# Message passes of a four-layer GNN: matrix building before the segment sums in PE's turn

## The chip, the cores and the metric

The kernel runs on one core of one Trainium2 chip. The metric is the time of one execution on the device, in microseconds (us). Lower is better. A core has five engines that work side by side and are ordered only by semaphores: TensorE (PE; the profile lists its weight loads apart, as PEld), VectorE (DVE), ScalarE (ACT), GpSimd (POOL) and SyncE (SP). Each runs its own instructions strictly in the order in which the kernel wrote them.

## The reference

A graph with 6250 nodes of 64 features and 206250 edges, sorted by destination, goes through four layers. Each normalizes the rows, applies relu, and adds the layer's result to x.

```python
h = relu(layernorm(x))
# L0: agg[dst] += h[src] @ W_msg + b_msg ; out = l2norm(agg + h @ W_self + b_self)
# L1: out[dst] += h[src] @ weight[edge_type]            (16 relations)
# L2: three hops: emb' [dst] += edge_weight * emb[src]  ; out = mean of the four emb
# L3: e = mlp(h_src, h_dst, edge_attr) ; out[dst] += e * (h @ W_src)[src] ; out += h @ W_tgt
```

So L0 and L1 each need one message pass: fetch a row of a table for every edge, and add the rows of the edges of one destination (a segment sum). L2 needs the same sparse matrix three times. The kernel therefore builds it once as dense chunks in DRAM (`B_d`) and multiplies by it.

## The kernel before

Edges lie in steps of 128 edges of one destination block. Eight steps (G = 8) are a group. A pass over all edges is 208 groups, 52 iterations of R = 4 turns, one group a turn. There are two message passes (0 for L0, 1 for L1), and in their turns the chunks of the L2 matrix are built as well. A chunk has 16 parts. Pass 0 builds 39 chunks with 3 parts in each of its 208 turns. Pass 1 builds the other 23 chunks with 2 parts in each of its first 184 turns. Its last 24 turns build nothing.

What one turn of group g consists of, engine by engine, each in this order in its own queue:

- POOL (`rows_of_group`, L497): waits for the group's indices (`idx_ok`), then issues eight indirect DMAs that gather 128 rows each into slot r of four in `gat`. After one turn in sixteen parts it also fetches a record for the matrix (`matrix_rows`, L506).
- PE (`segment.groups`, L884): waits for the group's gathers, for its one-hot matrix S (`S_ok`), and for the sum bank to be free (`acc_ok`), makes eight matmuls S x rows into bank 6 or 7 (16 instructions in the profile), and signals `mm_ok`. Then come the turn's matrix parts (`matrix_part`, L871): eight matmuls each (again 16 instructions), which wait for `lhs_ok` from DVE and, for the bank, for `bev` from ACT. Once a chunk, three transposes follow (`record_columns`, L862).
- DVE: the one-hot matrix of group g+1 (`one_hot`, L1190, which waits until segment sum g-1 is done), then for each part three instructions (`matrix_part`, L1228, L1229, L1231, the last one signals `lhs_ok`; the first waits until the matmuls of the part before last are done), once a chunk `record_weights` (L1209 to L1214), then `accumulate` (L1204): a wait for `mm_ok` of group g and eight additions of the sum bank into the accumulators.
- ACT: waits for `mm_ok` of group g and copies the indices of group g+4 for POOL (L683), then empties the banks of the turn's parts into `stg` (`matrix_part`, L671), once a chunk `columns_of` (L662).
- SP writes `stg` to `B_d` in quarters of a chunk (`matrix_out`, L420).

The order in each queue is written out by hand. `message_turns` runs all engines through the same turns: eight iterations (pass 0) or four (pass 1) are written out as one loop body. Between the passes `project` (L842) makes the second table.

Of the kernel before, what the change touches and what calls it, by code (L numbers as in the profile page):

```python
# [21 lines left out]
def gnn_kernel(nc, x, src, dst, edge_attr, etype, eweight, msg_wt, msg_b, self_wt, self_b, lin, rel_w,  # L22
# [51 lines left out]
    with ExitStack() as ctx:  # L74
# [207 lines left out]
        def wait(eng, semaphore, value):  # L282

            if not isinstance(value, int) or value > 0:
                eng.wait_ge(semaphore, value)
# [8 lines left out]
        def message_turns(n, eng, body):  # L294

            size, turn = BODY[n], PER_TURN[n]
            per_body = size * R * turn // SUBS

            def parts(b, k):
                at = [[(k * R + r) * turn + t for t in range(turn)] for r in range(R)]  # L300
                return [[(b * per_body + (FIRST[n] + o // SUBS), o % SUBS, (FIRST[n] + o // SUBS) % 2) for o in row] for row in at]

            def whole(b, count):
                for k in range(count):
                    body(b * size + k, parts(b, k))

            whole(0, size)
            with eng.Fori(1, BUILD_ITERS[n] // size) as b:
                whole(b, size)
            whole(BUILD_ITERS[n] // size, BUILD_ITERS[n] % size)  # L310
            if BUILD_ITERS[n] < ITER:
                none = [[] for r in range(R)]
                with eng.Fori(BUILD_ITERS[n], ITER - 1) as i:
                    body(i, none)
                body(ITER - 1, none)

        def next_chunk(row, pos):

            for c, at, h in row:
                if at == pos and not (isinstance(c, int) and c == NCH - 1):  # L320
                    return c + 1, 1 - h
            return None
# [221 lines left out]
        def _(act):  # L544
            parts = [0]
# [112 lines left out]
            def columns_of(c, h):  # L658

                act.wait_ge(s_["recT"], c + 1)  # L660
                wait(act, s_["lhs_ok"], (c - 1) * SUBS)
                act.copy(cols[:, h, :], ps[1][:, 0:3 * P]).then_inc(s_["cols_ok"], 1)  # L662

            def matrix_part(c, pos):

                act.wait_ge(s_["bmm"], c * SUBS + (pos + 1))
                r, j = pos // QS, pos % QS
                if j == 0:
                    wait(act, b_out[r % 2], c * 32 + r // 2 * 16)
                w = G // 2 * KC  # L670
                act.copy(stg[:, r % 2, j * w:(j + 1) * w], ps[3 + j % 2][:, 0:w]).then_inc(s_["bev"], 1)  # L671

            def message_pass(n, table):

                for r in range(R):
                    act.wait_ge(s_["mm_ok"], n * NG + r + 1)
                    act.copy(idx[:, r, :], table[:, r * G:(r + 1) * G]).then_inc(s_["idx_ok"], 1)

                def groups(i, parts):
                    for r in range(R):  # L680
                        if not (isinstance(i, int) and i == ITER - 1):
                            act.wait_ge(s_["mm_ok"], i * R + (n * NG + R + r + 1))
                            act.copy(idx[:, r, :], table[:, bass.ds((i * R + (R + r)) * G, G)]).then_inc(s_["idx_ok"], 1)  # L683
                        for c, pos, h in parts[r]:
                            matrix_part(c, pos)
                        ahead = next_chunk(parts[r], 9)
                        if ahead:
                            columns_of(*ahead)

                message_turns(n, act, groups)  # L690
# [95 lines left out]
        def _(pe):  # L786
# [69 lines left out]
            def record_columns(c, h):  # L856

                pe.wait_ge(s_["wm_ok"], c + 1)
                wait(pe, s_["cols_ok"], c)
                for f in range(3):  # L860
                    g0 = (0, 1, 3)[f] * P
                    ins = pe.transpose(ps[1][:, f * P:(f + 1) * P], recb[:, h, g0:g0 + P], ident[:])  # L862
                ins.then_inc(s_["recT"], 1)

            def matrix_part(c, j):

                pe.wait_ge(s_["lhs_ok"], c * SUBS + (j + 1))
                wait(pe, s_["bev"], c * SUBS + (j - 1))
                for t in range(G):
                    a, i2 = t % 2, t // 2  # L870
                    ins = pe.matmul(ps[3 + j % 2][a * KP:(a + 1) * KP, i2 * KC:(i2 + 1) * KC], Lw[:, j % 2, t, :], Rc[:, j % 2, t, :],  # L871
                                    start=True, stop=True)
                ins.then_inc(s_["bmm"], 1)

            def segment(n):

                def groups(i, parts):
                    for r in range(R):
                        pe.wait_ge(gather_ok[r], i * (16 * G) + (n * (NG // R) + 1) * 16 * G)
                        pe.wait_ge(s_["S_ok"], i * R + n * NG + r + 1)  # L880

                        wait(pe, s_["acc_ok"], (i * R + n * NG + r - 1) * G)
                        for k in range(G):
                            ins = pe.matmul(ps[6 + r % 2][:, k * D:(k + 1) * D], S[:, r % 2, k, :], gat[:, r, k * D:(k + 1) * D],  # L884
                                            start=True, stop=True)
                        ins.then_inc(s_["mm_ok"], 1)
                        for c, pos, h in parts[r]:
                            matrix_part(c, pos)
                        ahead = next_chunk(parts[r], 9)
                        if ahead:  # L890
                            record_columns(*ahead)

                message_turns(n, pe, groups)
# [518 lines left out]
```

## Time and profile before

| | |
|---|---|
| median of 3 runs | 8440.53 us (8440.46 to 8444.3) |
| profiled execution | 8453.61 us, span 8451.6 us, mean granted clock 0.665 |
| PE busy | 5784.8 us, 68% of the span |
| DVE busy | 4682.9 us, 55% |
| POOL busy | 4978.6 us, 59% |
| ACT busy | 1528.8 us, 18% |

The profile describes one execution. Busy times are sums over the span, so an engine that is the limit of one stage may look idle in the mean. The two message passes take slices 2 to 12 and 13 to 23 of the profile's 40 slices of 211 us each. A granted clock of 0.5 is TensorE's level of 1.2 GHz, 1.0 is 2.4 GHz, and values between are mixtures over the stretch.

### The profile page before, as it was taken

What the parts mean: (1) busy time and instruction counts of PE and PEld (TensorE: products, weight loads), DVE (VectorE), ACT (ScalarE), POOL (GpSimd) and SP (SyncE); (2) the same over time, 40 slices, a digit from 0 to 9 for tenths busy, and PEclk for the clock granted to TensorE, in tenths of its full rate; (3) what the DMA queues carried; (4) which work ended last, traced back from release to release, by engine and by line L of the source; (5) the groups of instructions that cost most, each with busy time, mean ns of one, the idle gap of its engine ahead of it and who ended that gap; (6) DMA issues with size and microseconds to landing.
All of it is one profiled execution on the core that took longest, in us unless ns stands there. A gap on an engine that the chain in (4) does not pass through costs nothing.

```text
span 8451.6 us, 133532 instructions
## 1 busy us (share of the span) xinstructions
PE 5784.8 (68%) x42197; PEld 4230.0 (50%) x42197; DVE 4682.9 (55%) x10280; ACT 1528.8 (18%) x4330; POOL 4978.6 (59%) x5265
## 2 busy tenths in 40 slices
PE   2476777777776555556554477777767788778877
PEld 2466666666644555555554222222235555555555
DVE  3688898998863667667664200000025555555555
ACT  1111111111122111111110000000013333333333
POOL 0577777777733777777777411111117777777776
PEclk6566556555555666666665699999976656665666
DMA  5655555555543444444442599999953333333332
GB/s 135 97 92 89 89 93 91 92 93 89 90 101 106 71 68 71 68 69 69 68 71 42 201 426 401 423 426 397 426 217 87 82 82 82 81 82 82 82 81 69
DMA packets 794607, 1178.96 MB, mean 139 GB/s; under 512 B 619664, under 2 KB 647729, under 8 KB 766544
## 3 DMA queue, kind: packets, MB, share of 16 engines
q1 hardware_dynamic: 616460, 919.49, 35.5%
q0 software_dynamic: 172528, 250.20, 16.2%
q8 instruction: 215, 3.52, 0.2%
q10 hardware_dynamic: 5204, 4.11, 0.2%
q14 instruction: 200, 1.64, 0.1%
HBM read 921.76 MB, written 258.23 MB: 140 GB/s over the span
## 4 chain that ended last, share of the span: by engine, by line
POOL 45%; issue 20%; DMA 16%; PE 12%; DVE 5%; ACTq 1%; DVEq 1%; POOLq 0%; ACT 0%; SPq 0%
POOL arena L497 44%; DMA arena<-B_d 12%; PE ps L931 5%; DMA arena<-tab,idx 2%; PE ps L842 2%; PE ps L884 2%; DVE ps L1228 1%; ACTq L279 1%; DMA arena<-rec_d,tcol 1%; DVE arena L1231 1%; DVE pair L1204 1%; PE ps L871 1%; PE ps L835 1%; DVE arena L1229 1%; POOL recb L506 1%
## 5 line engine op out<-in xcount | busy, mean ns | idle before, releaser
L497 POOL DMA_INDIRECT arena<-tab,idx x4992 | 4730.9, 948 | 1907.9 <-issue 1644.1
L884 PE MATMUL ps<-arena 128*128 128x64 f32 x6656 | 1351.6, 388 | 1088.0 <-DMA arena<-tab,idx 1010.2
L884 PEld LDWEIGHTS ps<-arena 128*128 128x128 f32 x6656 | 1288.0, 297 | 1172.0 <-issue 921.0
L871 PE MATMUL ps<-arena 128*64 128x98 f32 x15872 | 1368.0, 349 | 447.0 <-DVE arena L1231 440.3
L871 PEld LDWEIGHTS ps<-arena 128*64 128x64 f32 x15872 | 1152.4, 206 | 610.8 <-DVE arena L1231 548.0
L931 PE MATMUL ps<-arena,ev 128*64 128x512 f32 (+1 forms) x4836 | 1106.7, 603 | 370.8 <-DMA arena<-B_d 294.9
L1229 DVE TENSOR_TENSOR arena<-arena,ps 128x784 f32<-128x784 f32 x992 | 957.1, 965 | 0.0
L931 PEld LDWEIGHTS ps<-arena,ev 128*64 128x64 f32 x4836 | 383.9, 143 | 1093.3 <-issue 742.4
L534 POOL DMA_INDIRECT ev<-emb_d,dvI x186 | 175.1, 941 | 1259.5 <-PE ps L931 1041.4
L1190 DVE TENSOR_TENSOR arena<-relT,ps 128x1024 f32<-128x1024 f32 x624 | 759.3, 1217 | 201.7 <-issue 198.8
L1296 DVE COPY pair<-ps 128x512 f32<-128x512 f32 x9 | 5.7, 684 | 1437.4 <-PE ps L931 1437.4
L1228 DVE TENSOR_TENSOR ps<-arena,ps 128x512 f32<-128x512 f32 x992 | 682.7, 688 | 157.6 <-PE ps L871 155.9
L671 ACT COPY stg<-ps 128x392 f32<-128x392 f32 x992 | 481.3, 485 | 1426.7 <-PE ps L871 1411.7
L958 PE MATMUL ps<-ident,arena 128*64 128x128 f32 x3328 | 384.9, 406 | 446.7 <-DMA arena<-tab,idx 446.7
L1231 DVE TENSOR_TENSOR arena<-ps,arena 128x512 f32<-128x512 f32 x992 | 679.2, 685 | 5.3 <-issue 5.3
L958 PEld LDWEIGHTS ps<-ident,arena 128*64 128x64 f32 x3328 | 303.1, 209 | 708.1 <-DMA arena<-tab,idx 705.9
L1359 DVE TENSOR_TENSOR pair<-pair,ps 64x128 f32 x1664 | 475.2, 286 | 212.3 <-PE ps L993 121.2
L1204 DVE TENSOR_TENSOR X<-X,ps 128x64 f32 x832 | 183.8, 221 | 723.3 <-PE ps L884 698.0
L1204 DVE TENSOR_TENSOR pair<-pair,ps 128x64 f32 x2496 | 515.6, 220 | 69.7 <-issue 51.1
L1331 DVE TENSOR_TENSOR arena<-ps,stg 128x512 f32<-128x512 f32 x208 | 143.9, 692 | 660.7 <-ACT stg L759 657.0
L752 ACT COPY arena<-arena 128x192 bf16 x1664 | 440.4, 347 | 126.4 <-issue 126.4
L954 PE MATMUL ps<-stg,Web 17*128 17x512 f32 x416 | 350.1, 933 | 29.1 <-DMA stg<-attr_s 29.1
(213 smaller groups left out, 3889.2 us busy)
## 6 DMA issues: line engine op xcount, KB each, us to landing
arena<-B_d SPq DMA_DIRECT2D x186, 3136.0 KB, 17.2
B_d<-stg SPq DMA_DIRECT2D x248, 784.0 KB
arena<-tab,idx POOLq DMA_INDIRECT x4992
arena<-rel_d SPq DMA_DIRECT2D x208, 256.0 KB
tab<-arena SPq DMA_DIRECT2D x26, 1024.0 KB, 3.8
attr_s<-arena SPq DMA_DIRECT2D x13, 512.0 KB, 14.6
stg<-attr_s SPq DMA_DIRECT2D x208, 32.0 KB
emb_d<-pair SPq DMA_DIRECT2D x3, 1664.0 KB, 16.3
```

What stands on the lines that cost most here:

```text
L497: pool.indirect_dma_start(gat[:, r, k * width:(k + 1) * width], None, table, bass.IndirectOffsetOnAxis(ap=idx[:, r, k:k + 1], axis=0)).the ...
L671: act.copy(stg[:, r % 2, j * w:(j + 1) * w], ps[3 + j % 2][:, 0:w]).then_inc(s_["bev"], 1)
L871: ins = pe.matmul(ps[3 + j % 2][a * KP:(a + 1) * KP, i2 * KC:(i2 + 1) * KC], Lw[:, j % 2, t, :], Rc[:, j % 2, t, :], start=True, stop=True)
L884: ins = pe.matmul(ps[6 + r % 2][:, k * D:(k + 1) * D], S[:, r % 2, k, :], gat[:, r, k * D:(k + 1) * D], start=True, stop=True)
L931: ins = pe.matmul(ps[k][h * D:(h + 1) * D, 0:n], ev[:, u % EVS, :], Bb[:, u % BUFS, c0:c0 + n], start=c == 0, stop=c == NCH - 1)
L958: pe.matmul(ps[h][t * D:(t + 1) * D, q * P:(q + 1) * P], gv[:, r, k, D:2 * D], ident[:], start=False, stop=True, skip_group_check=True)
L1190: dve.tensor_tensor(S[:, h, :, :], steps_of(relT, g), iota_view(n, P), ALU.is_equal).then_inc(s_["S_ok"], 1)
L1204: dve.tensor_tensor(a, a, ps[6 + r % 2][:, k * D:(k + 1) * D], ALU.add).then_inc(s_["acc_ok"], 1)
L1228: dve.tensor_tensor(ohp, column(0, KP), iota_view(0, KP), ALU.is_equal).then_inc(s_["ohp_ok"], 1)
L1229: dve.tensor_tensor(Rc[:, j % 2, :, :], column(1, KC), iota_view(0, KC), ALU.is_equal)
L1231: dve.tensor_tensor(Lw[:, j % 2, :, :], ohp, column(2, KP), ALU.mult).then_inc(s_["lhs_ok"], 1)
L1359: dve.tensor_tensor(a, a, part, ALU.add).then_inc(s_["acc_ok"], 1)
```

## The change

In each turn of both message passes PE now makes the turn's matrix parts first and the group's segment sum after them. ACT empties the banks of these parts first, and waits for the segment sum and copies the indices after that. The orders of DVE, POOL and SP stay. No instruction is added or removed.

```diff
@@ ScalarE, groups(i, parts) @@
                     for r in range(R):
+                        for c, pos, h in parts[r]:
+                            matrix_part(c, pos)
                         if not (isinstance(i, int) and i == ITER - 1):
                             act.wait_ge(s_["mm_ok"], i * R + (n * NG + R + r + 1))
                             act.copy(idx[:, r, :], table[:, bass.ds((i * R + (R + r)) * G, G)]).then_inc(s_["idx_ok"], 1)
-                        for c, pos, h in parts[r]:
-                            matrix_part(c, pos)
                         ahead = next_chunk(parts[r], 9)
@@ TensorE, groups(i, parts) @@
                     for r in range(R):
+                        for c, pos, h in parts[r]:
+                            matrix_part(c, pos)
                         pe.wait_ge(gather_ok[r], i * (16 * G) + (n * (NG // R) + 1) * 16 * G)
                         pe.wait_ge(s_["S_ok"], i * R + n * NG + r + 1)
...
                         ins.then_inc(s_["mm_ok"], 1)
-                        for c, pos, h in parts[r]:
-                            matrix_part(c, pos)
                         ahead = next_chunk(parts[r], 9)
```

## Rows read from the trace of the kernel before

**Rows 1.** The page, busy tenths and granted clock in 40 slices.

```profile
DVE  3688898998863667667664200000025555555555
POOL 0577777777733777777777411111117777777776
PEclk6566556555555666666665699999976656665666
```

**Rows 2.** Source view of the gathers, pass 0: count, ns min/median/max, first and last start.

```profile
L497 POOL DMA_INDIRECT arena<-tab,idx x1664: 940/944/1058, 287.4 to 2412.3; - x185
```

**Rows 3.** The same for pass 1.

```profile
L497 POOL DMA_INDIRECT arena<-tab,idx x1664: 940/944/1062, 2635.4 to 4738.7; - x185
```

**Rows 4.** Timeline of pass 0 (start, us, engine, line; idle before).

```profile
2001.08 1.65 DVE L1204 TENSOR_TENSOR pair<-pair,ps 128x64 f32 x8
2002.72 3.68 PE L884 MATMUL ps<-arena 128*128 128x64 f32 x16
...
2009.44 0.69 DVE L1231 TENSOR_TENSOR arena<-ps,arena 128x512 f32<-128x512 f32 x1
...
2010.18 0.89 PE L871 MATMUL ps<-arena 128*64 128x98 f32 x16 [0.50 <-DVE arena L1231]
2010.25 1.66 DVE L1204 TENSOR_TENSOR pair<-pair,ps 128x64 f32 x8
...
2011.00 2.00 PE L884 MATMUL ps<-arena 128*128 128x64 f32 x16
...
2020.82 1.65 DVE L1204 TENSOR_TENSOR pair<-pair,ps 128x64 f32 x8 [0.95 <-issue]
```

**Rows 5.** Timeline of pass 1, two turns.

```profile
3402.77 3.67 PE L884 MATMUL ps<-arena 128*128 128x64 f32 x16 [8.99 <-DMA arena<-tab,idx]
...
3406.66 0.22 DVE L1204 TENSOR_TENSOR X<-X,ps 128x64 f32 x1 [7.00 <-PE ps L884]
...
3415.56 0.22 DVE L1204 TENSOR_TENSOR X<-X,ps 128x64 f32 x1 [0.96 <-issue]
...
3421.96 0.69 DVE L1231 TENSOR_TENSOR arena<-ps,arena 128x512 f32<-128x512 f32 x1
```

**Rows 6.** Timeline of pass 0, parts spaced by DVE.

```profile
1926.78 1.57 PE L871 MATMUL ps<-arena 128*64 128x98 f32 x16 [0.96 <-DVE arena L1231]
...
1928.28 3.68 PE L884 MATMUL ps<-arena 128*128 128x64 f32 x16
...
1933.99 1.57 PE L871 MATMUL ps<-arena 128*64 128x98 f32 x16 [0.50 <-DVE arena L1231]
...
1936.07 1.28 PEld L871 LDWEIGHTS ps<-arena 128*64 128x64 f32 x16 [0.80 <-DVE arena L1231]
```

**Rows 7.** Windows: us, then busy of PE, PEld, DVE, ACT, POOL, granted clock.

```profile
1930.00:1940.00 10.00, 6.64 (x58) 5.59 (x57) 7.56 (x17) 1.65 (x4) 7.56 (x9) 0.50 0.58 97
2010.00:2020.00 10.00, 5.95 (x72) 5.20 (x74) 9.70 (x23) 1.86 (x5) 7.54 (x8) 0.83 0.70 108
4600.00:4700.00 100.00, 36.71 (x160) 34.88 (x160) 28.44 (x90) 1.97 (x10) 75.48 (x81) 0.50 0.15 26
```

**Rows 8.** Groups by line, pass 0 (299 to 2428 us).

```profile
L871 PE MATMUL ps<-arena 128*64 128x98 f32 x9984 | 891.3, 355 | 374.9 <-DVE arena L1231 368.8 <-ACT stg L671 4.1 <-issue 0.7
L884 PE MATMUL ps<-arena 128*128 128x64 f32 x3328 | 667.8, 384 | 199.6 <-DMA arena<-tab,idx 137.9 <-issue 36.6 <-DVE arena L1190 16.1
...
L1228 DVE TENSOR_TENSOR ps<-arena,ps 128x512 f32<-128x512 f32 x624 | 429.8, 689 | 157.6 <-PE ps L871 155.9
L1204 DVE TENSOR_TENSOR pair<-pair,ps 128x64 f32 x1663 | 331.9, 220 | 61.9 <-issue 51.1 <-DVE pair L1204 7.8
```

**Rows 9.** Groups by line, pass 1 while it builds (2647 to 4500 us).

```profile
L884 PE MATMUL ps<-arena 128*128 128x64 f32 x2928 | 592.1, 386 | 735.5 <-DMA arena<-tab,idx 720.3 <-DVE arena L1190 6.9 <-DVE pair L1204 6.1
L871 PE MATMUL ps<-arena 128*64 128x98 f32 x5854 | 473.6, 340 | 72.1 <-DVE arena L1231 71.5
...
L1190 DVE TENSOR_TENSOR arena<-relT,ps 128x1024 f32<-128x1024 f32 x183 | 223.3, 1220 | 33.4 <-issue 31.9
```

## The prediction

> **What bounds the kernel now.** I read the 40 slices first, then the gathers, then two turns of the timeline, then the groups of each pass.
>
> In the slices of pass 0 (2 to 12) POOL stands at 7 while DVE stands at 8 or 9; in pass 1 (13 to 23) POOL again at 7, DVE at 6 or 7, with a granted clock of 0.6 in both [rows 1]. POOL's 7 is a full engine: the reader is to see that gathers run without a hole. In pass 0 1664 gathers start between 287.4 and 2412.3 us, together with 39 record gathers on the same engine: 2124.9 / 1702 = 1.248 us from start to start, of which 0.94 is busy and the rest is issue [rows 2]. Pass 1: 2103.3 / (1663 + 23) = 1.247 us [rows 3]. So POOL paces both passes, with 8 x 1.248 = 9.98 us for a group.
>
> DVE is close behind in pass 0. From one run of additions (L1204) to the next it takes 2010.25 - 2001.08 = 9.17 us, and a turn with a record has 1.4 more (10.57) [rows 4]. What matters is how it gets there: its additions need the segment sum of the same turn, and PE had made that sum (2.00 to 3.68 us) while DVE was building the turn's parts. DVE never waits for L884 in pass 0: its L1204 shows 61.9 us of idle time, none of it put down to PE [rows 8].
>
> **The change part by part.** *PE's order.* Segment sum g now stands behind the parts of turn g, the last of which waits for DVE's last L1231 of the turn. DVE's next instruction after that L1231 is the additions of g, which wait for segment sum g. Behind these additions in DVE's queue stand the one-hot matrix and all parts of the next turn, so nothing else can fill the wait; PE in turn then waits for the first of those parts. The two engines that overlapped now take turns. A turn is then a loop of five terms:
>
> 1. DVE, from its first addition to the end of the last L1231. Pass 0: 2009.44 + 0.69 - 2001.08 = 9.05 us [rows 4]. Pass 1, with two parts: 3421.96 + 0.69 - 3415.56 = 7.09 us [rows 5].
> 2. From there to PE's start: 2010.18 - 2010.13 = 0.05 us [rows 4].
> 3. The last part, to the start of the sum: 1928.28 - 1926.78 = 1.50 us at 1.2 GHz [rows 6], 2011.00 - 2010.18 = 0.82 at 2.4 GHz [rows 4].
> 4. The sum: 3.68 us or 2.00 us [rows 4].
> 5. From its end to DVE's first addition: 3406.66 - 3402.77 - 3.67 = 0.22 us [rows 5].
>
> Terms 2 to 5 come to 5.45 us at the low level and 3.09 us at the high one. A turn is 14.50 or 12.14 us in pass 0, and 12.54 or 10.18 us in pass 1. All are above POOL's 9.98, so POOL leaves the path and waits for indices instead.
>
> *Which level.* In the stretch 1930 to 1940 the parts start 2.08 us apart (1933.99, 1936.07), PE is idle for 0.5 us before each, and the clock stays at 0.50 [rows 6, 7]. That is the pattern of every turn after the change, since DVE makes a part in 2.08 us and PE no longer has a sum to catch up behind. Ahead of the first part PE will now always be idle for about 0.22 + 1.71 + 1.13 + 2.08, some 5.1 us. The stretch 2010 to 2020, with 0.83, follows PE work without such holes: sum, part and part nearly back to back. Segment sums alone, 3.67 of every 10 us, stay at 0.50 [rows 7]. So I take nine turns in ten at the low level: 14.50 - 0.1 x 2.36 = 14.26 us in pass 0, 12.54 - 0.24 = 12.30 us in pass 1.
>
> The Trainium skill (TensorE: Matmul & The Clock Gate, the HAM clock gate) says that the throttled clock is the default and that sustained activity releases it. A turn's PE work will be some 9 us long with holes of only 0.5 us, so by that rule the sum at its end would run at 2.4 GHz. That is a result of its own, and it stands among the rivals; the row of 1930 to 1940 speaks against it.
>
> *Records.* In 39 turns of pass 0 and 22 of pass 1, `record_weights` and the wait behind it cost DVE 1.4 us today. Now they lie in DVE's wait of 3.1 to 5.5 us for PE: no cost. PE's transposes follow the sum and lie in its idle time. If PE were done earlier than that, they would cost 39 x 1.4 = 55 us; I count nothing.
>
> *Stalls that POOL's pace hid.* DVE has idle time that no semaphore ends: in pass 0 some 33 us beside the record turns, worked out as the 70 us on its rows of "issue" less 39 x 0.95; in pass 1 31 us, nearly all ahead of L1190 [rows 8, 9]. In a serial loop they count: +33 and +31. PE has 36.6 us of the kind ahead of L884 in pass 0 [rows 8]; they may count too or fall into its idle time. I count none and keep 37 us for the upper end.
>
> *What goes.* DVE's 155.9 us of waiting for the banks of parts (L1228 on L871), which come from PE standing at a late gather, and PE's 137.9 and 720.3 us of waiting for gathers [rows 8, 9], vanish. They bring nothing: POOL hid them, and what is late next is the DVE and PE loop.
>
> *ACT's order.* Indices for group g+4 still leave right after sum g, because ACT waits for `mm_ok` in either order and the parts' banks are by then empty but for the last, 0.5 us. POOL then needs 10 us plus landing, and the group is used more than three turns (over 37 us) later: hidden. It would cost only if the gathers needed more than that. The bounds are 0 and, if those 0.5 us fell on POOL's path in each of 408 turns, 200 us; they are hidden while a turn is longer than 9.98 us. Taken: 0.
>
> *Sum.* Pass 0: 208 x 14.26 + 33 = 2999 us against 2428 - 298 = 2130 before: +869. Pass 1: 184 x 12.30 + 31 = 2294 us for the turns that build. Of the last 24, four have their gathers ready and twenty are paced by POOL: 20 x 9.98 + 10 = 210. That is 2504 against 2103 before (2647 to 4750): +401. Everything else, the hops and the edge layer included, is untouched. In all +1270 on the profiled execution: 8453.6 + 1270 = 9724 us. The median of the runs is 13 us below the profiled time, so 9711; I say 9710 us.
>
> **The rivals.**
> *A, the clock as it is now.* If the clock keeps today's shares, the means of the groups hold: a sum takes 667.8 / 208 = 3.21 us and a part 1.43 in pass 0; 592.1 / 183 = 3.24 and 1.29 in pass 1 [rows 8, 9]. With 0.07 off the part as in term 3, turns are 9.05 + 0.05 + 1.36 + 3.21 + 0.22 = 13.89 and 11.82 us, the passes 2922 and 2416: +792 and +313, 9545 us. For it: one slice is much like another today. Against: today's high stretches need work that the new order spreads out.
> *B, every sum at 2.4 GHz.* 208 x 12.14 + 33 = 2558 and 184 x 10.18 + 31 + 210 = 2114: +428 and +11, 8880 us. For it: the long activity ahead of each sum. Against: the stretch at 0.50 that has just that spacing.
> *C, POOL still paces (not slower).* One mechanism: with parts first, a late gather no longer holds up the parts, DVE runs ahead of PE, and the four gather slots take up the rest, so that each turn stays at POOL's 9.98 us. The place is DVE's wait ahead of L1204. The price is the loop of five terms, and it decides from where that falls under 9.98 us. Then the time stays at 8440 us; the ends of the passes could bring some 10 us either way. For it: pass 1 at the high level is at 10.18, nearly there. Against: pass 0 is 2 us above at any level, and DVE's queue leaves nothing to run ahead with. For the whole kernel it needs terms 3 and 4 to vanish.
>
> **How the numbers follow.** Forecast 0.70 (9600 to 9840 us on its own: all turns at the low level with PE's stalls is 208 x 14.50 + 33 + 37 = 3086 and 184 x 12.54 + 31 + 210 = 2548, so +956 and +445, 9841). A 0.19, between 9450 and 9600. B 0.08, C 0.03. The range that leaves out about two in ten, from the low side of A to the all-low sum, is 9450 to 9840 us. Against C this makes slower 0.97, same 0.02, faster 0.01. (0.2%, 17 us, is about what a measurement of this kernel can tell from no change.)
>
> **What would show it.** Right: in pass 0, DVE's L1204 waits for PE's L884 in nearly all 208 turns, some 4 to 5.4 us each, near 1000 us in all; PE's L871 waits for DVE's L1231 with one gap of about 5 us and two of 0.5 us a turn; POOL's L497 shows 4 us of idle time a turn ended by ACT's index copy, and PE no longer waits for gathers; the clock in slices of pass 0 reads 5, not 6. The first L1204 of two turns stand about 14.3 us apart in pass 0 and 12.3 in pass 1, and the last 24 turns stay at 10.0. The hops and the edge layer keep their lengths. Wrong: if the passes are long but L1204 does not wait for L884, the loop is another; if PE waits for gathers while POOL waits for indices, the four slots are too few; if the clock reads 6 or more, A or B.

## The result and the profile after

The changed kernel takes 9659.63 us (median; 9657.76 to 9662.04) against 8440.78 us: the ratio is 1.1443, with a 95% interval of 1.1423 to 1.1463. The profiled execution has a span of 9660.2 us at a mean clock of 0.616. The forecast was 9710 us, in a range of 9450 to 9840.

First the 40 slices of the page; one slice is now 241.5 us.

```profile
DVE  3566666666666445555555552000001555555555
POOL 0555555555555056566655665111110677777776
PEclk6555555555555555555555555999998666666666
```

POOL has gone from 7 to 5 and 6 and DVE from 8 or 9 to 6 in pass 0 [rows 1]: no engine is full in the passes any more, which is how a chain that goes back and forth between engines looks. The slices of the hops (9) and of the edge layer (6) read as before.

The clock's digits say little: in pass 0 the kernel before already reads 5 in eight of its eleven slices, and 6 in three [rows 1]; the changed kernel reads 5 throughout both passes. The windows of both (third figure from the right, the kernel before first) show that the granted clock fell from 0.60 to 0.54 in pass 0. In the building turns of pass 1 it fell from 0.62 to 0.51.

```profile
300.00:2428.00 2128.00, 1567.19 (x13429) 1391.36 (x13428) 1886.36 (x3898) 361.25 (x867) 1597.61 (x1693) 0.60 0.56 90
```
```profile
300.00:3200.00 2900.00, 1633.68 (x13246) 1423.13 (x13247) 1872.88 (x3859) 357.91 (x858) 1590.26 (x1685) 0.54 0.32 66
```

The source view of DVE's additions gives the ends of both passes and what they waited for. The kernel before, pass 0, then pass 1 with its last turns (count; ns min/median/max; first and last start):

```profile
L1204 DVE TENSOR_TENSOR pair<-pair,ps x1663: 209/220/223, 307.0 to 2427.9; 128x64 f32 x185
```
```profile
L1204 DVE TENSOR_TENSOR X<-X,ps x832: 209/222/223, 2650.4 to 4749.2; 128x64 f32 x167
  PE ps L884: 698.0, 125
```

The changed kernel, pass 0 and pass 1:

```profile
L1204 DVE TENSOR_TENSOR pair<-pair,ps x1664: 214/221/223, 301.6 to 3223.7; 128x64 f32 x185
  PE ps L886: 1015.0, 208
...
L1204 DVE TENSOR_TENSOR X<-X,ps x832: 213/221/223, 3446.0 to 5960.1; 128x64 f32 x167
  PE ps L886: 1123.6, 208
```

Pass 0 grew from 2120.9 to 2922.1 us (+801.2) and pass 1 from 2098.8 to 2514.1 (+415.3). The start is 5.4 us earlier. That makes +1211 of the +1208.6 us between the spans; all else stayed within 3 us. DVE waits for the segment sum (L886, formerly L884) in all 208 turns of each pass. It never did so in pass 0 before [rows 8], and 125 times in all before.

Two turns of pass 0 after, a selection of rows from the timeline (start, us; idle time before, and what ended it):

```profile
1802.22 0.68 DVE L1231 TENSOR_TENSOR arena<-ps,arena 128x512 f32<-128x512 f32 x1
1802.95 1.57 PE L871 MATMUL ps<-arena 128*64 128x98 f32 x16 [0.50 <-DVE arena L1231]
1804.46 3.68 PE L886 MATMUL ps<-arena 128*128 128x64 f32 x16
1808.37 1.65 DVE L1204 TENSOR_TENSOR pair<-pair,ps 128x64 f32 x8 [5.47 <-PE ps L886]
...
1813.41 1.58 PE L871 MATMUL ps<-arena 128*64 128x98 f32 x16 [5.28 <-DVE arena L1231]
1815.48 1.57 PE L871 MATMUL ps<-arena 128*64 128x98 f32 x16 [0.50 <-DVE arena L1231]
1816.83 0.68 DVE L1231 TENSOR_TENSOR arena<-ps,arena 128x512 f32<-128x512 f32 x1
1817.56 1.56 PE L871 MATMUL ps<-arena 128*64 128x98 f32 x16 [0.50 <-DVE arena L1231]
1819.05 2.00 PE L886 MATMUL ps<-arena 128*128 128x64 f32 x16
1821.28 1.66 DVE L1204 TENSOR_TENSOR pair<-pair,ps 128x64 f32 x8 [2.93 <-PE ps L886]
```

Read it as one chain: DVE's last L1231 ends at 1802.90, PE's last part starts 0.05 us later, the sum behind it ends at 1808.14, DVE's additions start at 1808.37. DVE has stood still for 5.47 us. Then PE stands still for 5.28 us until DVE has made the next part. The second turn's sum ran at 2.4 GHz (2.00 us), and its wait is 2.93 us.

POOL, from the source view of its gathers in pass 0:

```profile
L497 POOL DMA_INDIRECT arena<-tab,idx x1664: 938/944/962, 277.6 to 3178.8; - x185
  ACT idx L685: 833.6, 199
```

POOL lost its pace [rows 2]: it waits 833.6 us for indices, in 199 turns. PE no longer waits for a gather in the turns of pass 0. In pass 1 it waits for gathers ahead of its first sum and in the last 20 turns, where no parts are built.

### The profile page after: what moved, and what is told of

Same layout as the page of the kernel before. It is cut to its first block, busy times and chain, and to the rows that moved or that the text cites. A ratio compares the mean times of both kernels' runs of the same rounds, so it can differ in the third digit from the quotient of the medians.

```text
span 9660.2 us, 133531 instructions
## 1 busy us (share of the span) xinstructions
PE 6025.0 (62%) x42197; PEld 4379.8 (45%) x42197; DVE 4693.4 (49%) x10280; ACT 1529.7 (16%) x4330; POOL 4979.7 (52%) x5265
## 4 chain that ended last, share of the span: by engine, by line
PE 28%; DVE 23%; issue 17%; POOL 14%; DMA 13%; DVEq 3%; ACTq 1%; ACT 0%; POOLq 0%; SPq 0%
POOL arena L497 14%; PE ps L886 14%; DMA arena<-B_d 10%; DVE ps L1228 7%; PE ps L871 6%; DVE arena L1231 6%; PE ps L931 4%; DVE pair L1204 4%; DVE arena L1229 4%; DVEq L1196 2%; PE ps L842 2%; DVE arena L1190 1%; ACTq L279 1%; DVE X L1204 1%; DVEq L1204 1%
## 5 line engine op out<-in xcount | busy, mean ns | idle before, releaser
L871 PE MATMUL ps<-arena 128*64 128x98 f32 x15872 | 1545.7, 374 | 2367.2 <-DVE arena L1231 2349.2
L871 PEld LDWEIGHTS ps<-arena 128*64 128x64 f32 x15872 | 1251.3, 222 | 2630.5 <-DVE arena L1231 2392.2
L886 PE MATMUL ps<-arena 128*128 128x64 f32 x6656 | 1420.2, 402 | 141.1 <-DMA arena<-tab,idx 139.1
L886 PEld LDWEIGHTS ps<-arena 128*128 128x128 f32 x6656 | 1345.9, 309 | 232.4 <-issue 188.5
L1204 DVE TENSOR_TENSOR pair<-pair,ps 128x64 f32 x2496 | 517.9, 221 | 1033.0 <-PE ps L886 1015.0
L1190 DVE TENSOR_TENSOR arena<-relT,ps 128x1024 f32<-128x1024 f32 x624 | 759.0, 1217 | 204.7 <-issue 201.8
L1204 DVE TENSOR_TENSOR X<-X,ps 128x64 f32 x832 | 183.8, 221 | 1127.8 <-PE ps L886 1123.6
L1231 DVE TENSOR_TENSOR arena<-ps,arena 128x512 f32<-128x512 f32 x992 | 676.2, 682 | 0.0
```

What stands on the lines that cost most here:

```text
L1190: dve.tensor_tensor(S[:, h, :, :], steps_of(relT, g), iota_view(n, P), ALU.is_equal).then_inc(s_["S_ok"], 1)
L1204: dve.tensor_tensor(a, a, ps[6 + r % 2][:, k * D:(k + 1) * D], ALU.add).then_inc(s_["acc_ok"], 1)
L1231: dve.tensor_tensor(Lw[:, j % 2, :, :], ohp, column(2, KP), ALU.mult).then_inc(s_["lhs_ok"], 1)
```

## The experiments

**Each half and each pass.** The first leaves PE as it was and moves only ScalarE's copy of the indices.

```diff
 # act_only: ScalarE as in the change, PE as before
+ for c, pos, h in parts[r]: matrix_part(c, pos)
  act.wait_ge(mm_ok, ...); act.copy(idx ...)
- for c, pos, h in parts[r]: matrix_part(c, pos)
```

> ScalarE's half alone: it empties the turn's banks first and copies the indices after that, while PE keeps the segment sum ahead of the parts. Theory 1 (DVE and PE take turns: DVE's additions wait for a sum that stands behind the parts): 8440 us within 20, because PE's order is as before and the indices, some 5 to 6 us later a turn, are still ahead of POOL. Theory 2 (the cost comes from indices that leave later, so that POOL's gathers start later): most of the +1219 us is already here, 9400 us or more, with POOL's gathers waiting for L685's copy several us a turn.

Measured: 8440.01 us, ratio 0.9999 (0.9989 to 1.0008). With PE's order as before, later indices cost nothing. POOL's gathers wait for the copy in 22 turns, 6.7 us in all:

```profile
  ACT idx L685: 6.7, 22
```

So POOL's 833.6 us of waiting in the changed kernel is a consequence of the long turn, not its cause. PE's half alone was not run: in pass 0 the third part of a turn waits until ScalarE has emptied the first one's bank, and ScalarE would wait for a sum behind that third part. That is why the change has two halves.

```diff
 # pass1_only / pass0_only: both halves under  if n == 1:  /  if n == 0:
```

> Both halves of the change, in message pass 1 alone. Theory 1: pass 1 goes from 2100 to about 2513 us and pass 0 stays near 2125: 8440 + 415 = 8855 us (8830 to 8880). If the cost of the two passes depended on one another (tables, matrix writes), it would be off by more than 30.

Measured: 8858.73 us, one run: +417.6.

> Both halves of the change, in message pass 0 alone. Theory 1: 8440 + 802 = 9242 us (9215 to 9270), and with the kernel that changes pass 1 alone it adds up to the whole change. Pass 0's additions wait for the sum about 1000 us in all.

Measured: 9272.56 us, one run: +831, a little over the stated span. The two add up to +1249, 30 us over the whole change. The difference lies where the clock acts: worked out from the clock's records between the first and last additions of pass 0, its high share was 0.06 here and 0.083 in the changed kernel. A sum took 3.36 us here in the mean against 3.28, and a turn 14.22 against 14.11. With one run each, why the clock was lower here stays open. Pass 1 took the same time in this kernel as before.

**DVE's wait one turn later.**

```diff
 # late_add: the changed kernel, DVE's turn (conditions at the first and last group left out)
-    one_hot(n, g + 1, (r + 1) % 2)
     for c, pos, h in parts[r]: matrix_part(c, h, pos)
     record_weights(...)
-    accumulate(n, i, r, acc)
+    accumulate(n, i, r - 1, acc)      # the group before
+    one_hot(n, g + 1, (r + 1) % 2)
```

> The changed kernel, orders of PE and ACT as changed, but DVE's turn is: parts, additions of the group before, one-hot matrix of the next group. So DVE waits for a segment sum one turn later. Theory 1: the loop of five terms is cut, DVE's wait for L886 goes from 2140 us to under 300, POOL paces again: 8440 to 8550 us. Theory 2 (indices late): indices still leave after the sum behind the parts, so it stays near 9650. Theory 3 (the lower clock of PE makes the loss): PE's work and its place behind the parts stay, the clock stays at 0.6 or below, and the time stays over 9300.

Measured: 8442.95 us, ratio 1.0001 (0.9992 to 1.0011). The whole cost is gone with PE's and ScalarE's orders untouched. The timeline shows why:

```profile
1806.82 3.67 PE L886 MATMUL ps<-arena 128*128 128x64 f32 x16 [0.85 <-DMA arena<-tab,idx]
...
1810.42 3.08 PE L871 MATMUL ps<-arena 128*64 128x98 f32 x32
...
1811.22 0.68 DVE L1231 TENSOR_TENSOR arena<-ps,arena 128x512 f32<-128x512 f32 x1
...
1814.13 1.64 DVE L1204 TENSOR_TENSOR pair<-pair,ps 128x64 f32 x8
1814.27 0.89 PE L871 MATMUL ps<-arena 128*64 128x98 f32 x16 [0.77 <-DVE arena L1231]
```

The sum that ran from 1806.82 to 1810.49 is added at 1814.13, after DVE has built three parts beside it. Round the loop the order is again that of the kernel before: sum g, the parts that DVE builds after one-hot g+1, additions of g. Only the part numbers are shifted by one group. What the change broke is the distance between a sum and its additions.

One part of the expectation missed: DVE's wait for the sums is 732.4 us, not under 300. That is the wait of the kernel before (698.0 us), nearly all of it in pass 1, where gathers come late at POOL's pace; the change's own wait is gone. The clock over pass 0 is back at 0.59, so this run alone does not tell the loop from the lower clock of theory 3; one_ahead, below, does.

**How many parts ahead.** One or two of the turn's parts before the sum, the rest behind it, on PE and ScalarE alike.

```diff
 # one_ahead (k = 1), two_ahead (k = 2)
+ for c, pos, h in parts[r][:k]: matrix_part(c, pos)
  ... segment sum / copy of the indices ...
- for c, pos, h in parts[r]: matrix_part(c, pos)
+ for c, pos, h in parts[r][k:]: matrix_part(c, pos)
```

> One part of the turn ahead of the segment sum, the others behind it (PE and ACT alike). Theory 1 by the five terms: while PE does the first part and the sum (5.45 us at 1.2 GHz), DVE still has two parts of 2.08 us to build in pass 0 and one in pass 1. Wait left: 1.3 us in pass 0 (turn 10.35, POOL 10.2) and 3.4 us in pass 1 (turn 10.46, POOL 10.1), less at 2.4 GHz. So 8460 to 8560 us, a twentieth of the change's cost, not a third. A theory in which the cost is per part moved would give 8440 + 1219 x 392/992 = 8920 us or so.

Measured: 8529.29 us, ratio 1.0107 (1.009 to 1.0123): small, but clear of noise.

> Two parts ahead of the segment sum, so pass 1 is as in the changed kernel and pass 0 has one part behind the sum. Theory 1: pass 0's turn is 9.05 + 5.45 - 2.08 = 12.42 us at 1.2 GHz, 10.2 at 2.4 GHz: +380 to +490 us there, +415 in pass 1: 9235 to 9345 us.

Measured: 9302.54 us, ratio 1.102 (1.1001 to 1.1038).

The mean turns, worked out from the first additions of each group, are 10.33 and 10.63 us for one part (expected 10.35 and 10.46) and 12.37 us in pass 0 for two (expected 12.42). So the cost is not one per part moved. It is what is left of 5.45 us after the parts that DVE still builds beside PE, and it starts where a turn passes POOL's 10.2 us: the first part costs 86 us, the second 773, the third, which only pass 0 has, 357.

one_ahead also shows that a lower clock alone does not make the loss. Its sums took 3.51 us in the mean in pass 0 and 3.68 in pass 1, longer than in the changed kernel (3.28 and 3.53), and its granted clock over the building turns of pass 1 was 0.50. Even so it lost 86 us, not 1219. What a low clock costs depends on how much of PE's work DVE waits for.

**The length of the sum.**

```diff
 # double_sum: the changed kernel, every sum of a building turn made twice
- for k in range(G):
+ for k in (list(range(G)) + list(range(G)) if parts[r] else range(G)):
```

> The changed kernel with every segment sum of a turn that builds made twice over (16 matmuls, same result). Theory 1: the whole sum lies in the loop, so each of 392 turns grows by one sum, 3.3 to 3.7 us at 1.2 GHz: +1300 to +1440 us, 10960 to 11100 us, and DVE's wait for the sum grows by as much. A theory in which part of the sum is hidden (by DVE's work or by POOL's 9.98 us) gives less than +1000 us.

Measured: 10881.51 us, one run, +1222 to the changed kernel. DVE's additions now wait for L886:

```profile
  PE ps L886: 3364.0, 416
```

That is 1225 us more than the 2138.6 before, the same as the growth of the time. So every added microsecond of the sum lies in the loop. The stated size was too high, since I took nearly all added sums at 1.2 GHz: the two sums took 6.25 us together in pass 0 and 6.88 in pass 1, so the second one added 2.97 and 3.35 to the 3.28 and 3.53 of the changed kernel. The 1000 us bound of the rival is passed all the same.

**The clock.** Extra matmuls of a part's form in PE's holes.

```diff
 # fill: the changed kernel; fill_all also has the last line (shortened)
  ... segment sum ...
+ pe.wait_ge(cols_ok, ...)      # ScalarE has read the columns out of bank 1; in fill_all ahead of the parts
+ 24 x pe.matmul(ps[1][a*KP:(a+1)*KP, 3*P:3*P+KC], ident[:, 0:KP], ident[:, 0:KC])   # a = 0, 1, 0, ...
+ behind every part of a turn but the last: 4 x the same
```

> The changed kernel with 24 extra matmuls of a part's form (ident times ident into unused columns of bank 1, result not used) behind each segment sum of a turn that builds. They take about 4.7 us at 1.2 GHz and 2.7 at 2.4 GHz, in a hole of 5.2 us in which PE now waits for DVE. If the clock answers to PE's activity as in the trace of before (it rose behind back-to-back parts), last part and sum run at 2.4 GHz in most turns: pass 0's turn falls from 14.1 to about 12.2 us, pass 1's from 12.5 to 10.3: 8850 to 9050 us although work is added. If the level does not change: 9660 to 9750 us.

Measured: 9572.88 us, ratio to the kernel before 1.1338 (1.1319 to 1.1357): 87 us faster than the changed kernel, not 600. The clock over pass 0 rose from the 0.54 of the changed kernel to 0.68, but in the wrong place.

```profile
300.00:3220.00 2920.00, 2194.53 (x23236) 1976.26 (x23236) 1879.18 (x3868) 359.96 (x863) 1585.69 (x1681) 0.68 0.35 66
```

A turn of its timeline (L895 are the extra matmuls):

```profile
1804.90 4.19 PE L895 MATMUL ps<-ident 128*64 128x98 f32 x48
...
1810.25 0.90 PE L871 MATMUL ps<-arena 128*64 128x98 f32 x16 [1.16 <-DVE arena L1238]
...
1812.33 1.03 PE L871 MATMUL ps<-arena 128*64 128x98 f32 x16 [1.18 <-DVE arena L1238]
...
1814.40 1.58 PE L871 MATMUL ps<-arena 128*64 128x98 f32 x16 [1.04 <-DVE arena L1238]
...
1815.91 3.68 PE L886 MATMUL ps<-arena 128*128 128x64 f32 x16
```

In this turn the clock is high for the first part and the start of the second, which nobody waits for, and low for the last part and the sum. PE had been idle for 1.16 and 1.18 us ahead of the first two parts.

Pass 0, in spite of its higher clock, gained nothing: its mean turn is 14.14 us against 14.11, and 17% of its sums took under 2.4 us, against 24% in the changed kernel. The whole gain is in pass 1, 87.5 us between its first and last additions. There 24% of the sums of building turns took under 2.4 us, against 9%, and the mean turn fell from 12.54 to 12.06 us.

> As fill, and 4 more extra matmuls (0.4 to 0.8 us) behind every part of a turn but the last, so that PE is also busy in the holes of 0.5 to 1.2 us between the parts, just ahead of the sum. In fill the clock's high share rose to 0.36 and 0.39, but the sum still took 3.36 and 3.24 us: the level had fallen again while parts waited for DVE. If what counts is PE's work just ahead of the sum, the high level now reaches last part and sum in most turns: sums near 2.2 us, turns near 12.3 and 10.4 us, 8900 to 9100 us in all. If the holes between parts are not the reason: the sum stays above 3.2 us, and the time is 9550 to 9700 us.

Measured: 9187.19 us, ratio 1.0875 (1.0857 to 1.0893): 472 us faster than the changed kernel, with more work on PE. Pass 0 is 258 us shorter than in the changed kernel and pass 1 217. The granted clock of pass 0 is 0.82:

```profile
300.00:2960.00 2660.00, 1937.88 (x26574) 1770.30 (x26570) 1883.39 (x3875) 360.40 (x863) 1589.60 (x1684) 0.82 0.39 73
```

The sums of both fills between 297 and 3000 us, which is all of pass 0 in fill_all and 190 of its 208 sums in fill, from the groups by line, fill first (here L886, in fill_all L898):

```profile
L886 PE MATMUL ps<-arena 128*128 128x64 f32 x3040 | 643.7, 399 | 0.0
```
```profile
L898 PE MATMUL ps<-arena 128*128 128x64 f32 x3328 | 481.4, 305 | 0.0
```

A sum went from 643.7 / 190 = 3.39 to 481.4 / 208 = 2.31 us, and 82% of the sums of pass 0 took under 2.4 us, 72% in pass 1. The direction was right, the size fell short (8900 to 9100 expected): mean turns are 12.86 and 11.35 us, since the other 18% and 28% of the sums did not run at 2.4 GHz throughout.

fill_all changes two things at once, the place and the amount of the added work. The small groups without the 24 matmuls were not run, nor were 28 or 32 matmuls in the long hole alone. That the place counts, and not only the amount, is argued from fill's pass 0, where a clock of 0.68 brought nothing; it is not shown by itself.

**DVE's later additions with PE's old order.**

```diff
 # late_add_before: the kernel before with late_add's DVE turn
```

> DVE's turn as in late_add (parts, additions of the group before, next one-hot matrix), with PE and ACT in the order of the kernel before. By theory 1 POOL paces it as it paces before: 8440 us within 25; DVE's wait for sums in pass 1 (523 us before) shrinks, which brings nothing.

Measured: 8539.84 us, ratio 1.0117 (1.0101 to 1.0134). I had expected no change, and this missed. The one-hot matrix now comes last in DVE's turn, PE's next sum needs it, and DVE's third part in turn needs a bank that PE frees only behind that sum. Waits of pass 0 (us in total, times, longest):

```profile
PE ps L884 <- DVE arena L1190: 340.1, 191, 4.8
DVE ps L1228 <- PE ps L871: 258.4, 199, 6.0
```

It is a second loop of the same kind, with a median turn of 10.25 us before records against 9.98 for POOL, so it shows only in pass 0 (mean turn 10.67, against 10.24 in the kernel before; pass 1 stays at 10.13). PE's instructions in this loop ran at the low level: the sums of pass 0 took 3.64 us in the mean, against 3.21 in the kernel before.

## Why the prediction was right

*The loop of five terms* holds, term by term. In the mean of all turns after the first of a pass, worked out from the starts and ends of the instructions (us; pass 1 without its last 24 turns):

| | pass 0 | pass 1 |
|---|---|---|
| DVE, first addition to the end of the last L1231 | 9.12 | 7.23 |
| to PE's start | 0.06 | 0.05 |
| last part, to the start of the sum | 1.43 | 1.50 |
| the sum | 3.28 | 3.53 |
| to DVE's first addition | 0.22 | 0.22 |
| turn | 14.11 | 12.54 |

The median turns are 14.51 and 12.45 us; I had 14.50 and 12.54 for the low level. The count of parts ahead and the doubled sum bear out that nothing of the last part and the sum is hidden.

*The level of the clock* was the term that was mis-sized, in both directions. That one turn in ten would run at 2.4 GHz was a guess. By the starts and ends of its instructions, 24% of pass 0's sums and 9% of pass 1's took under 2.4 us. The forecast's last part and sum come to 4.94 us in both passes; they took 4.71 and 5.04. With the stalls that I added, its turns were 14.42 and 12.47 us. Pass 0 was 0.31 shorter: 0.23 by the clock, the rest mostly by stalls that did not come. That is 64 of the 68 us by which it was forecast too long (+869 against +801). Pass 1 was 0.07 longer, 13 of the 14 us by which it was forecast too short. The two misses have opposite signs, so a little of the nearness of 9710 to 9660 is luck.

*The clock's digits* were misread. The prediction says 0.6 for both passes of the kernel before, and takes a 5 in pass 0 as a sign that it is right and a 6 as a sign of rival A or B. Most slices of pass 0 read 5 already, so this sign could not tell the forecast from A.

*Rival A*, the clock's shares as before, came nearer than the forecast in pass 0. The granted clock over the pass fell, but 24% of the sums took under 2.4 us before the change as well, and a sum took 3.21 us in the mean before and 3.28 after. A had +792 us for the pass; +801 was measured. In pass 1 it fails: the share fell from 23% to 9%, a sum took 3.53 us and not 3.24, and +415 was measured where A had +313. *Rival B*, every sum at 2.4 GHz, did not come about: some 9 us of PE work with holes of 0.5 us kept the low level in most turns, as the stretch of [rows 6, 7] had. When fill_all put work into these holes, and into the long one, 82% and 72% of the sums took under 2.4 us. The Trainium skill (TensorE: Matmul & The Clock Gate, A second HAM failure mode: psum-queue depth-cycling) tells of another kernel, in which short idles of PE between groups of matmuls come often enough to make the clock oscillate. The trace of fill agrees in kind: three parts of one turn, each behind a hole of 1.0 to 1.2 us, took 0.90, 1.03 and 1.58 us. *Rival C*, POOL still paces, would need turns of 9.98 us. No building turn was shorter than 10.38 us; only the last 20 turns of pass 1, without parts, kept POOL's pace, as the forecast had it.

*Records* cost nothing more, as argued: the 39 turns of pass 0 with a record took 14.09 us in the mean, the others 14.12. *Stalls:* PE's 36.6 us ahead of the sum fell away (0.0 idle time ahead of L886 in pass 0). Of DVE's, those ahead of L1204 went into its wait, and those ahead of L1190 stayed (13.3 us in pass 0, 35.0 in pass 1). I had counted 33 and 31. *DVE's waits for banks* (155.9 us) and PE's for gathers in building turns vanished and brought nothing. *ScalarE's order* costs 0, measured alone with PE's old order.

## What to carry to other kernels

When two engines feed each other, draw one turn as a loop and count what each still has to do between giving and needing. A result that is used on the other side straight after it is made puts both engines in series, though each looks half idle in the profile. Moving an instruction behind work that waits for the other engine costs little while the other engine still has work to do beside it, and its full length once that work is used up, not a share per piece: here one part ahead cost 86 us and the second 773. The same loss can be undone on the other side of the loop, by using the result one turn later, if nothing else in that turn is then made too late.

## What the runs showed of the hardware

Work added to PE made the changed kernel faster by 472 us, because the sum on the path ran at 2.4 GHz in most turns (2.31 us in the mean of pass 0 for 3.28). A higher mean clock alone is not a gain: 24 matmuls in the long hole raised the granted clock of pass 0 from 0.54 to 0.68 and left its turn at 14.1 us, since the sums there were no faster (3.36 us); the 87 us that they gave came from pass 1. With 4 more behind each part but the last, 8 a turn in pass 0 and 4 in pass 1, the clock of pass 0 was 0.82, and the time fell by another 385 us.
